# A new order of every engine's list in a gated cross-attention block, and 34 unread products ahead of a weight sum

## The reference

```python
def _quant_weight(w):
    scale = jnp.mean(jnp.abs(w)) + EPS
    wq = jnp.clip(jnp.round(w / scale), -1.0, 1.0)
    return (wq, scale)

def _quant_act(x):
    s = jnp.max(jnp.abs(x), axis=-1, keepdims=True) / 127.0 + EPS
    xq = jnp.clip(jnp.round(x / s), -128.0, 127.0)
    return (xq, s)
...
qp = q @ Wq.T + bq;  kp = k @ Wk.T + bk            # q = k = ctx
scores = (qp @ kp.T) * H**-0.5 * layernorm(x)      # masked with -inf
x = x + tanh(g_xattn[0]) * softmax(scores)
...
gate = silu(qlinear(layernorm(x), w_gate));  up = qlinear(layernorm(x), w_up)
x = x + tanh(g_ffn[0]) * qlinear(gate * up, w_down)   # 512 -> 2048 -> 512
```

## Time and profile before

| | us |
|---|---|
| median of 3 runs (lowest, highest) | 224.48 (224.33, 224.86) |
| span of the profiled execution | 222.5 |
| TensorE busy | 199.3 (90%) |
| VectorE busy | 180.2 (81%) |
| ScalarE busy | 124.5 (56%) |
| POOL busy | 97.8 (44%) |

### The profile page before, as it was taken

One profiled execution on the slowest core, in us unless ns is written; L12 is line 12 of the kernel. 1 busy time (PEld: TensorE's weight loads), 2 busy tenths in 40 slices (PEclk: granted clock), 3 DMA queues, 4 the chain that ended last, 5 costly groups with the idle time before them and its releaser, 6 DMA issues.

```text
span 222.5 us, 2846 instructions
## 1 busy us (share of the span) xinstructions
PE 199.3 (90%) x854; PEld 90.3 (41%) x854; DVE 180.2 (81%) x359; ACT 124.5 (56%) x165; POOL 97.8 (44%) x154
## 2 busy tenths in 40 slices
PE   8764008999999998999999999999999999999994
PEld 7221004344444344444444444444444444444441
DVE  0598979799989799797997989888898987888721
ACT  2179998999895952246964414896413035453000
POOL 2629743593764955320499204135973312020200
PEclk9995555899999999999999999999999999999999
DMA  6999999790022577300235640343607830540592
GB/s 215 420 423 423 417 391 424 281 325 8 3 47 47 115 186 172 98 0 3 47 64 121 153 91 15 69 80 74 141 3 175 201 89 13 96 79 16 97 188 94
DMA packets 47360, 32.84 MB, mean 148 GB/s; under 512 B 40944, under 2 KB 41072, under 8 KB 45808
## 3 DMA queue, kind: packets, MB, share of 16 engines
q1 hardware_dynamic: 47200, 32.51, 50.4%
q10 hardware_dynamic: 144, 0.13, 0.3%
HBM read 18.48 MB, written 4.19 MB: 102 GB/s over the span
## 4 chain that ended last, share of the span: by engine, by line
PE 71%; DMA 14%; ACT 5%; DVE 4%; issue 2%; SPq 2%; DVEq 0%
PE pU L947 23%; PE pG L934 23%; PE pD L965 20%; DMA stage_b<-in_L_ffn_w_up 8%; DMA stage_a<-in_L_ffn_w_down 4%; PE pA L909 3%; ACT down_w L689 2%; DMA stage_b<-stage_b 2%; ACT L736 1%; ACT hid L736 1%; DVE abs_part L1345 1%; SPq L351 1%; PE pA L898 1%; ACT stage_b L743 1%; DVE am L1320 1%
## 5 line engine op out<-in xcount | busy, mean ns | idle before, releaser
L736 ACT ACTIVATE hid<-pG,act_g 128x512 f32<-128x512 f32 x64 | 43.6, 688 | 54.6 <-PE pG L934 54.4
L934 PE MATMUL pG<-gate_w,xqT 128*128 128x512 f16 x256 | 64.7, 388 | 1.4 <-DVE xqT L1303 0.8
L947 PE MATMUL pU<-up_w,xqT 128*128 128x512 f16 x256 | 62.7, 379 | 0.0
L965 PE MATMUL pD<-down_w,stage_b 128*128 128x512 f16 x256 | 57.3, 379 | 0.6 <-DMA stage_b<-stage_b 0.6
L1311 DVE TENSOR_TENSOR hid<-pU,hid 128x512 f32<-128x512 f32 x64 | 43.6, 685 | 11.1 <-PE pU L947 9.2
L934 PEld LDWEIGHTS pG<-gate_w,xqT 128*128 128x128 f16 x256 | 25.1, 100 | 37.0 <-issue 8.0
L965 PEld LDWEIGHTS pD<-down_w,stage_b 128*128 128x128 f16 x256 | 24.9, 98 | 31.8 <-issue 2.3
L947 PEld LDWEIGHTS pU<-up_w,xqT 128*128 128x128 f16 x256 | 25.1, 98 | 31.3 <-issue 1.7
L743 ACT ACTIVATE stage_b<-hid,inv 128x1024 f16<-128x1024 f32 x15 | 16.9, 1139 | 7.8 <-DVE inv L1329 7.8
L560 POOL TENSOR_SCALAR out_scale<-den,act_e,down_k 128x1 f32<-128x1 f32 x16 | 5.9, 371 | 33.4 <-DVE den L1326 33.4
L909 PE MATMUL pA<-kT,qT 128*128 128x512 f32 x26 | 15.4, 678 | 4.9 <-ACT kT L709 4.9
(11 more groups left out here) (96 smaller groups left out, 236.1 us busy)
## 6 DMA issues: line engine op xcount, KB each, us to landing
stage_a<-in_L_ffn_w_gate SPq DMA_DIRECT2D x4, 1024.0 KB, 11.2
stage_b<-in_L_ffn_w_up SPq DMA_DIRECT2D x4, 1024.0 KB, 19.2
stage_a<-in_L_ffn_w_down SPq DMA_DIRECT2D x4, 1024.0 KB, 9.0
stage_b<-in_x SPq DMA_DIRECT2D x2, 1024.0 KB, 5.3
out<-x SPq DMA_DIRECT2D x8, 256.0 KB, 2.4
out<-stage_b SPq DMA_DIRECT2D x8, 256.0 KB, 2.4
ctx_s<-in_ctx SPq DMA_DIRECT2D x4, 256.0 KB, 14.4
x<-in_x SPq DMA_DIRECT2D x2, 512.0 KB, 5.8
```

The source lines that it names most:

```text
L736: act.activation(hid[:, t % NH, n * 512:(n + 1) * 512], pG[c % NG][:, :], ACT.Silu, scale=act_g[:, t:t + 1]).then_inc(silu_done, 1)
L934: ins = pe.matmul(pG[c % NG][:, :], xqT[:, t // TILES % 2, t % TILES, k, :], gate_w[:, n, k, :], start=k == 0, stop=k == KD - 1)
L947: ins = pe.matmul(pU[c % NU][:, :], xqT[:, t // TILES % 2, t % TILES, k, :], up_w[:, n, k, :], start=k == 0, stop=k == KD - 1)
L965: ins = pe.matmul(pD[t % ND][:, :], hidT[:, t % 2, k, :], down_w[:, k // KD, k % KD, :], start=k == 0, stop=k == KI - 1)
```

## The change

1. Every engine's list has a new order, and the tables that give steps to engines are new. The gate and up chunks of tiles 2 and 3 are numbered in pairs, as those of tiles 0 and 1 were.
2. Projections and scores use other banks: query and key of batch 0 no longer share one (the key goes to pG0), the query of batch 1 goes to pG1 and its key to pG0, scores 0 to 2 to the three banks of pU. q_ready and k_ready are a semaphore for each batch.
3. SP loads the masks behind x tiles 0 to 3 and the second context, x of batch 1 (tiles 4 to 7) behind the first gate chunk, x of batch 2 ahead of the down weights, and the fourth down chunk behind the transpose of tile 4.
4. Sums of absolute values come in pieces: the fourth gate chunk in two halves on ScalarE, the fourth up chunk in one half on VectorE and one on ScalarE. VectorE rounds gate chunk 0 and down chunk 2 itself. POOL's rounding no longer waits for the bound of the chunk before it.
5. The exp's bias is one operation behind the maximum (the negative of the inverse deviation is made ahead), and VectorE makes the gate factors of a group at once.
6. `keep(n)` multiplies constant ones, 34 products of 128 x 128 in all, into pU1, in TensorE's list between score(4) and weight_sum(0). Nothing reads them.

```diff
 def chunk(t, n):
-    return 2 * n + t if t < 2 else NC * t + n
+    return 2 * NC * (t // 2) + 2 * n + t % 2 if t < TILES else NC * t + n
...
-        first_banks = [pA, *pU, pD[-1]][:TILES]
+        q_banks = [pA, pG[1], pA, pA]
+        k_banks = [pG[0], pG[0], pA, pA]
+        score_banks = [*pU, pA]
...
-        RESIDUAL_BY = "VPVVPPPPPPPVPPPP"
+        RESIDUAL_BY = 'VPPVPPPPPVPPPPVP'
...
-        ABS_BY = ["AAAV", "AVAA", "AAAA"]
-        SIGN_BY = ["QXXX", "QQQX", "XXQQ"]
+        ABS_PIECES = [[(0, 0, 2048, 'A'), (1, 0, 2048, 'A'), (2, 0, 2048, 'A'), (3, 0, 1024, 'A'), (3, 1024, 2048, 'A')], [(0, 0, 2048, 'A'), (1, 0, 2048, 'A'), (2, 0, 2048, 'A'), (3, 0, 1024, 'V'), (3, 1024, 2048, 'A')], [(0, 0, 2048, 'A'), (1, 0, 2048, 'A'), (2, 0, 2048, 'A'), (3, 0, 2048, 'A')]]
+        SIGN_BY = ['VQQQ', 'QXQX', 'XQVQ']
...
+                pool.wait_ge(rstd1_ready, g + 1)
+                pool.tensor_scalar(nrstd1[:, t0:t1], rstd1[:, t0:t1], -1.0, 1.0, ALU.mult, ALU.mult)\
+                    .then_inc(nrstd1_done, 1)
...
-                pool.tensor_scalar(nmx[:, t0:t1], mx[:, t0:t1], -1.0, 1.0, ALU.mult, ALU.mult).then_inc(nmx_done, 1)
-                pool.wait_ge(nmx_done, g + 1)
-                pool.wait_ge(rstd1_ready, g + 1)
-                pool.tensor_tensor(negb[:, t0:t1], nmx[:, t0:t1], rstd1[:, t0:t1], ALU.mult).then_inc(negb_ready, 1)
+                pool.wait_ge(nrstd1_done, g + 1)
+                pool.tensor_tensor(negb[:, t0:t1], mx[:, t0:t1], nrstd1[:, t0:t1], ALU.mult).then_inc(negb_ready, 1)
...
-                if m or n:
-
-                    wait_ternary(pool, *divmod(NC * m + n - 1, NC))
...
+            def keep(n):
+                pe.wait_ge(scored, 2)
+                for _ in range(n):
+                    pe.matmul(pU[1][:, 0:P], ones[:, :], ones[:, :], start=True, stop=True)
...
             def project_k(b):
-                pe.wait_ge(q_ready, b + 1)
-                pe.matmul(pA[:, :], wk_s[:, :], ctx_s[:, b % NQ, :], start=True, stop=True).then_inc(k_done, 1)
+                if b >= 2:
+                    wait_pA(pe, "k", b)
+                elif b == 1:
+                    pe.wait_ge(k_ready[0], 1)
+                pe.wait_ge(ctx_loaded[b], 16)
+                pe.matmul(k_banks[b][:, :], wk_s[:, :], ctx_s[:, b % NQ, :], start=True, stop=True).then_inc(k_done, 1)
...
+            def weight_round(m, n):
+                dve.wait_ge(winv_done, m + 1)
+                dve.tensor_scalar(chunk_of(m, n), stages[m][:, n, :], winv[:, m:m + 1], None, ALU.mult)\
+                   .then_inc(w_round_dve, 1)
...
             score(4)
+            keep(8)
+            keep(9)
+            keep(8)
+            keep(9)
             weight_sum(0)
```

More of the change, by code:

```diff
@@ L815, in _ @@
             silu(6, 0)
+            quantise_x(7)
+            silu(6, 1)
+            silu(6, 2)
+            silu(6, 3)
             exp(8)
@@ L1034, in _ @@
             up(3, 3)
+            gate(4, 0)
+            up(4, 0)
+            up(4, 1)
+            gate(4, 1)
+            score(8)
+            gate(4, 2)
+            up(4, 2)
+            gate(4, 3)
+            weight_sum(2)
+            up(4, 3)
+            up(5, 0)
+            gate(5, 0)
+            gate(5, 1)
+            up(5, 1)
+            down(0, 0)
+            down(0, 1)
+            gate(5, 2)
+            gate(5, 3)
+            down(1, 0)
             down(0, 2)
+            score(9)
             down(0, 3)
-            down(1, 0)
             down(1, 1)
+            score(10)
             down(1, 2)
+            up(5, 2)
+            gate(6, 0)
+            gate(6, 1)
+            score(11)
+            gate(6, 2)
+            gate(6, 3)
+            up(5, 3)
+            up(6, 0)
+            gate(7, 0)
+            gate(7, 1)
             down(1, 3)
@@ new lines, in _ @@
+            product(4, 2)
+            inverse_std2(3)
+            weight_scale(2)
+            absmax_hidden(2, 1)
+            weight_round(2, 2)
+            weight_bound(2, 0)
+            weight_bound(2, 1)
+            product(4, 3)
+            reciprocal_scale(1)
+            weight_bound(2, 2)
+            weight_bound(2, 3)
+            absmax_x(6)
+            absmax_x(7)
+            inverse_x(3)
+            stats1(10)
+            stats1(11)
+            inverse_hidden(2)
+            score(9)
@@ new lines, in _ @@
+            absmax_hidden(7, 1)
+            score(13)
+            absmax_x(11)
+            inverse_x(5)
+            inverse_hidden(6)
+            inverse_hidden(7)
+            product(8, 2)
+            product(8, 3)
+            residual2(4)
+            score(14)
+            mask_and_max(13)
+            residual2(5)
+            product(9, 0)
+            product(9, 1)
+            reciprocal_scale(4)
+            mask_and_max(14)
+            product(9, 2)
+            product(9, 3)
```

1041 lines of the change are left out of this document (505 added, 536 removed).

## The result

The changed kernel takes 226.83 us (median of four, 225.94 to 227.65) and the kernel before 224.52 beside it (224.33 to 224.86): a ratio of 1.0107, 95% interval 1.0078 to 1.0136. It is 1.1% slower; the prediction said 217.1 and gave slower 0.07. The profiled execution has a span of 225.8 us, where before had 222.5. A few executions (one of an experiment at 253 us, three of the kernel before at 231, 278 and 741) lie far above the rest and are left out of the medians and ratios.

What follows compares the result with a forecast made beforehand. A head chain delays TensorE, which bounds the body: first gate 29.6, content 179.0, head waits 0.9, half clock 1.2, body idle 1.2, tail 3.2, outside the span 2.0, making 217.1 us; range 214.9 to 221.5.

Steps and rivals of the forecast that it cites:

- the tail: Behind the last product at 211.9: 3.2 us as before, giving a span of 215.1.
- Loads: Head: x of the second batch lands at 14.05 instead of 33.6, every weight load after it 2.5 us later.
- The 34 products: Between score 4 and the gate sum: hidden at 0.12 to 0.13 us a record, by themselves worth 0 to 0.5 us.
- The chain of the head: Score, mask, exp, residual, statistics, absolute maximum, quantise: first gate chunk at 29.6, 5.6 us earlier.
- the walk: Each engine's new list carried forward with the trace's durations and spacings; a start is the later of engine and operand.
- the port lock: Head: VectorE's two-port forms and GpSimd exclude each other; rounding behind POOL's scales makes the first gate up to 1 us later.
- After the first gate: To 52.0: TensorE does 21 chunks and other work, 21.5 us of 22.4, so 0.9 of waits.
- Half clock: First gates: the clock falls before them and returns 4 to 5 us into them, costing about 1.2 us.
- The down stage: Down chunks start at 77, just when their weights are bounded (76.9).
- rival c: Slower: fourth down load late behind tile 4's transpose, stopping TensorE at the down sum; past 224.5 from 9.5 us slip; chance 0.07.
- The rest: Body: idle time as before, 1.2 us, with nothing there changing the bound.
- Rival (a): Products take 0.19 or more, or port lock bites: gate scale and all behind 1.5 to 4.6 us late, 218.6 to 221.7; chance 0.16.

Runs made afterwards that it cites:

- the improved kernel: Changed kernel with POOL's waits back, batch 1's mask later, gate chunk 1 rounded by ScalarE, down chunks 0 and 1 bounded before VectorE's rounding: 222.90 us, 0.9932.
- the two shorter executions: The lower pair among the changed kernel's four times, 225.94 and 226.05 us; the other pair is 227.61 and 227.65.

## Why the prediction was wrong, point by point

The profiled execution took 227.6 us, 10.5 more than the sum of the prediction: 2.4 at the first gate (32.04 for 29.6), 8.2 from there to the last product (190.5 for 182.3), the tail as said (3.2), and 0.2 less outside the span (1.8 for 2.0).

**Loads: right.** The statistics of tiles 4 and 5 did not wait for x, at 15.96 and 16.77.

**The 34 products: right.** 68 records in 7.75 us, 0.114 each (0.12 to 0.13 was taken, bounds 0.107 to 0.236); the gate sum at 24.27 (23.8); the clock at half in the window 30 to 35, and back before 37. They are worth 0.4 us in the improved kernel, inside the intervals, where 0 to 0.5 was said; in the changed one the difference is 1.1 (226.83 against 227.91, intervals that overlap), of which 0.9 is the bound that met a rounding in one trace and not in the other. The estimate from the Trainium skill ("TensorE: Matmul & The Clock Gate", Back-to-back issue gap), 81 ns a pair and doubled, would have given 11.0 us; the trace has 7.75, and it decides.

**The chain of the head: 2.4 us too short.** The step used durations of instructions that ran alone. Measured against it: the first mask 1.57 for 0.68, the centring 1.43 for 0.48, the residual 1.17 for about 0.75, so 2.3, and 0.55 of wait for POOL's quantised tile in front of score 4, a dependency that the walk had missed (score 4 is written where POOL reads tile 0). A little of this was slack. By stages, measured against the walk: the exps end at 18.25 (17.4), POOL's second residual at 23.10 (22.0), the statistics at 25.30 (23.35), VectorE's score at 28.96 (26.4). VectorE's rounding, for which no row stood, was right: 1.29 for 1.3. The prediction had the earlier trace rows (1.22 beside POOL, 0.72 later), named the port lock, and gave it "up to 1 us" at one place, the rounding, where it did not strike. The experiment with the mask moved confirms 0.9 of it.

**After the first gate: waits of 0.9 predicted, 3.8 measured** (+2.9). This is the step that failed most. It let VectorE's bounds take 0.6 and POOL's roundings 1.97 in parallel. And it had no term for one line of the diff, the wait that POOL's rounding lost: the front section of this document quotes it, and the prediction never prices it. That wait was an ordering, not only a dependency: with it POOL rounds while VectorE does something else. The two experiments with it show its price: 2.1 us by the medians (1.3 against the two shorter executions) in the new order, and 1.3 in the old one. The scale of the up weights was made at 41.49, where the kernel before had it at 36.06, and by 52 us TensorE had done 13 chunks, not 21.

**Half clock: 1.2 predicted, 2.1 measured** (+0.9): the first two gate chunks took 3.57 for the 1.89 of later ones, and the score behind them 1.42 for 1.02. Holding the clock there gave no time, so as a cause this term is empty: what it doesn't cost is spent in waits.

**The down stage: nothing predicted, 3.8 measured** (+3.8): holes of 0.75 and 1.32, and 0.4 + 1.3 for a clock that fell again, the latter in the longer executions alone. The prediction had the down weights bounded "at 76.9, just when" they were needed, and looked for trouble at the load (rival c), which was innocent. The same lock, on a long rounding placed ahead of two bounds, was the cause of the holes; moving it gave 2.0 us back by the medians, 1.2 against the two shorter executions.

**The rest**: +0.6 us. The walk took 1.2 of idle time for the whole body; the trace has 0.51 before the last 24 products and hardly any other hole, but each of its seven holes also costs the tail of the product in front of it, 0.16, which the sum, made of steady products, doesn't have.

2.9 + 0.9 + 3.8 + 0.6 = 8.2, and 2.4 ahead of it. **Rival (a)** named the right mechanism and priced it at 1.5 to 4.6 us for a late start alone; **rival (c)** had the right sign by the wrong mechanism, and the chance of 0.07 for slower rested on it alone.

**Open**: in the improved kernel the first gate is still 1.8 us later than predicted, 3.6 us of holes stand before 52 us and 1.5 in the down stage. The largest, 1.77 before the first up chunk, stands behind a POOL rounding of 2.80 and VectorE's bound; 0.83 of the 2.80 are lost beside VectorE's masks at 40.70 and 41.31. Whether another engine for that rounding, or the masks behind it, closes the hole wasn't tried. Nor is it shown why the clock fell a second time in one trace of the changed kernel and not in the one with the down load moved, whose two holes are nearly the same (0.64 and 1.32), or in those with the mask moved and with ScalarE rounding (0.76 and 1.32 both): the link from the holes to the fall is open.

## What to carry to other kernels

When a change removes a wait between VectorE and GpSimd, price what the wait kept apart: an overlap of two instructions that exclude each other costs VectorE the rest of POOL's instruction, here up to 1.8 us for a bound of 0.68. Walk a new order with the durations that the trace shows for overlapping pairs, not those of instructions alone, and put first in VectorE's list what TensorE waits for. Work that only moves a start earlier pays where the operands behind it are earlier too: here 3.1 us of earlier start ended in holes, and a clock held at full did as well.

## What the runs showed of the hardware

- The exclusion is complete within what the records resolve. VectorE's tensor_scalar in f16, 128x2048, takes 0.68 us alone and 2.1 to 2.5 beside POOL's rounding of 1.97; the custom mask instruction (two inputs in SBUF) 0.68 alone, 1.57 beside POOL's mask conversion and 2.36 beside a rounding. Those of the changed kernel worked out here ended 0.53 to 0.55 us after POOL's instruction.
- It strikes POOL as well, when VectorE is first: two roundings back to back took 4.45, 4.87 and 5.40 us instead of 3.94, and small instructions on two columns went from 0.71 to 1.20 (rstd) and 1.27.
- Adding a wait made the kernel 2.1 us faster by the medians, and VectorE's busy time 191.3 us became 188.0 with the same work: part of what a profile calls busy is waiting for the port.
- f32 products of 128 x 128 columns in a stream take 0.114 us a record at the full clock, 0.236 in the warm-up of the earlier trace rows, where the page prints the full clock too. A projection's record took 1.17 right behind that warm-up and a score's 0.59 later, so the duration of a record is the better witness.
